# Attention and mixture-of-experts block: scores in tiles of 32 keys, one merging copy for each pair, expert regions in the sorted rows, the first norm on ScalarE, and a new instruction order

## The chip, the cores and the metric

The kernel runs on one core of a Trainium2 chip. The metric is the device time of one launch in microseconds (us), the median of several runs. Engines are called as the profile calls them: PE (TensorE matmul), PEld (its weight loads), DVE (VectorE), ACT (ScalarE), POOL (GpSimd), SP (SyncE, which only issues DMAs here).

## The reference

One transformer block over 4 batches of 1024 tokens, 128 features wide, all in float32:

```python
mod = (silu(c) @ wmod)                      # per batch: sa, ca, ga, sb, cb, gb
h = layernorm(x) * (1 + ca) + sa
# attention: 16 query heads, 4 key/value heads of 64, window of 128 keys, causal
scores = 30 * tanh((q @ k.T) / 8 / 30); mask = (j <= i) & (j > i - 128)
x = x + ga * (softmax(where(mask, scores, -1e30)) @ v) @ Wo.T
h = layernorm(x) * (1 + cb) + sb
# experts: 8, each takes the first C = 512 of the 4096 tokens whose largest gate is its own
gates = softmax(h @ Wg); e = argmax(gates); loc = how many earlier tokens chose e
out_t = gate_t * (relu(h @ W1[e] + b1[e]) @ W2[e] + b2[e]) if loc < 512 else 0
x = x + gb * out
```

## The kernel before

The 4096 tokens are 32 tiles of 128. A tile's queries meet the keys of its own tile and of the tile before it; tiles 0, 8, 16 and 24 (the first of each batch) have no tile before.

**First norm and projections, per pair of tiles.** DVE measures x (`measure1`, `gather1`), POOL makes the reciprocal deviation (`rstd1_of`), DVE writes the normalised tile XN (`normalise1`, L851), PE turns it (`turn_x`), ACT and DVE split it into a high and a low part XH and XL (`high_x`, `full_x`, `low_x`), and PE projects q (four groups), k and v in three float32r passes each (L343 to L345, L373 to L375).

**Scores.** `score(t, h)` makes the scores of one tile for two of its four key/value heads, transposed: keys on partitions, 4 heads by 128 queries in each of two banks. The scores of the own tile go to the two banks `own`, of which there is one pair only; those of the tile before go partly to `own` and partly to two of the six banks `turns` (the use is called "before"), in ten matmuls over 64x64 tiles of the array (L423 to L432). DVE then copies what belongs to the tile before over `own` where a triangular mask says so (`merge`, two predicated copies of 64 partitions, L869). A key of the own tile and one exactly 128 before it share a place, so the probabilities need one set of columns alone. ACT makes tanh (`weigh`, L688) and exp (`expose`, L694); the next `score` waits for that tanh, since it writes the same `own`.

**Weighted values.** `attend(t)` multiplies all probabilities PR by the values of the tile before (V) or by a mix of both tiles (VM, built by two DMAs of SP, `mix_v`), L461, and then adds a correction, the masked probabilities PM (POOL, `mask`, L1224) by the difference VD of the two tiles' values (POOL, `differ`), L468. It does so for the first 32 of each head's 64 value columns and then for the other 32. V matmuls use 128x32 tiles of the array, corrections 64x32 tiles. `sums(t)` (L482) adds up the probabilities, DVE inverts and spreads the sums (`turn_sums`, `invert`, `spread`) and scales (`scale`, L900), ACT and POOL split the result (`high_o` L700, `low_o` L1232), and `out_project` (L495 to L497) works on a pair of tiles.

**Second norm, gates and slots, per tile.** PE turns y back (`turn_y`, L504), DVE adds x (L911), measures, normalises and modulates (L917 to L937), PE turns the result (`turn_h2`, L510) and scores the experts (L516). DVE finds the largest (`top8`, `which`), writes a one-hot row (`mark`, L958), PE counts earlier tokens of the same expert (`count`, L524), DVE reads the count (`locate`, L968), makes slot = expert * 512 + count (`find_slot`, L973), an overflow term that moves a token past the end when its count is 512 or more (`find_over`, L978) and their sum as an integer (`number_slot`, L984). POOL scatters the row to `sorted_rows` by an indirect DMA (`scatter`, L1260); rows past the end are dropped. `sorted_rows` has 4096 rows and is filled with empty rows at the start by one DMA of 6400 KB.

**Experts.** From 433 us on the sorted rows are read back and PE works through the eight experts.

Each engine runs its instructions in the order written. For the first stage that order is written out by hand in one loop an engine, one pass for every two tiles: for instance `for e in range(-4, TILES + 8, 2)` on PE, with calls such as `score(e, 0)` and `attend(e - 2)` in it. Which of the six banks `turns` a use takes stands in the table `HOME`, and PE waits before a use until the bank's former user has read it (`freed`). On SP, `mix_v` waits behind the load of all first expert weights (L274) at the start.

## Time and profile before

| what | us |
|---|---|
| median of 3 runs (508.32 to 510.79) | 510.23 |
| profiled execution, whole | 510.57 |
| its span, first to last instruction | 508.8 |
| PE busy | 434.4 (85%) |
| DVE busy | 367.5 (72%) |
| ACT busy | 286.5 (56%) |
| POOL busy | 287.5 (57%) |

Busy is the time in which at least one instruction of the engine runs. Since one pass of the loops handles two tiles, the first stage repeats itself about every 25 us; a stretch of one such length, looked at instruction by instruction on each engine, says more than the totals. Weight loads overlap the matmuls.

### The profile page before, as it was taken

What the parts mean: (1) busy time and instruction counts of PE and PEld (TensorE: products, weight loads), DVE (VectorE), ACT (ScalarE), POOL (GpSimd) and SP (SyncE); (2) the same over time, 40 slices, a digit from 0 to 9 for tenths busy, and PEclk for the clock granted to TensorE, in tenths of its full rate; (3) what the DMA queues carried; (4) which work ended last, traced back from release to release, by engine and by line L of the source; (5) the groups of instructions that cost most, each with busy time, mean ns of one, the idle gap of its engine ahead of it and who ended that gap; (6) DMA issues with size and microseconds to landing.
All of it is one profiled execution on the core that took longest, in us unless ns stands there. A gap on an engine that the chain in (4) does not pass through costs nothing.

```text
span 508.8 us, 13662 instructions
## 1 busy us (share of the span) xinstructions
PE 434.4 (85%) x4936; PEld 286.6 (56%) x4936; DVE 367.5 (72%) x1061; ACT 286.5 (56%) x505; POOL 287.5 (57%) x398
## 2 busy tenths in 40 slices
PE   2884999899989898999898989989998951699980
PEld 1651666465656565556565655656564541599970
DVE  4272667888998989799989898898778844155541
ACT  3662656576766666665747485747666422455520
POOL 4151547476657575857575757557566853035672
PEclk9997999999999999999999999999999975799995
DMA  9985010101010101001010201020202103991110
GB/s 260 373 277 166 3 27 3 48 6 50 12 55 19 49 19 54 28 23 56 13 59 7 62 11 50 1 65 4 64 11 60 39 26 105 360 329 42 37 42 19
DMA packets 31961, 37.35 MB, mean 73 GB/s; under 512 B 3372, under 2 KB 28267, under 8 KB 31896
## 3 DMA queue, kind: packets, MB, share of 16 engines
q1 hardware_dynamic: 28824, 28.22, 17.9%
q0 software_dynamic: 3072, 8.28, 4.5%
q8 instruction: 40, 0.66, 0.5%
q14 instruction: 25, 0.20, 0.1%
HBM read 15.88 MB, written 17.31 MB: 65 GB/s over the span
## 4 chain that ended last, share of the span: by engine, by line
PE 63%; issue 13%; DVE 13%; DMA 4%; POOL 3%; ACT 2%; another core or an unknown queue 1%; POOLq 0%; SPq 0%; DVEq 0%; ACTq 0%
PE turns L461 7%; PE turns L482 6%; PE own L423 5%; PE turns L343 4%; PE turns L624 4%; PE turns L468 4%; PE turns L345 4%; PE turns L344 4%; PE turns L430 3%; PE turns L495 3%; PE turns L497 2%; PE turns L496 2%; DMA VM<-V 2%; DVE own L869 2%; DVE R L890 2%
## 5 line engine op out<-in xcount | busy, mean ns | idle before, releaser
L1224 POOL TENSOR_SCALAR_AFFINE_SELECT PM<-PR 128x1024 f32<-128x1024 f32 x64 | 70.0, 1094 | 72.3 <-ACT PR L694 72.2
L869 DVE COPY_PREDICATED own<-before,turns 64x512 f32<-64x512 uint32 x112 | 77.9, 695 | 30.7 <-PE own L432 28.6
L1232 POOL TENSOR_TENSOR OL<-O,OH 128x512 fp32r<-128x512 f32 x64 | 80.7, 1284 | 34.1 <-ACT OH L700 33.5
L688 ACT ACTIVATE PR<-own 128x1024 f32<-128x1024 f32 x64 | 65.4, 1021 | 60.4 <-DVE own L869 58.9
L694 ACT ACTIVATE PR<-PR 128x1024 f32<-128x1024 f32 x64 | 67.3, 1054 | 0.5
L423 PE MATMUL own<-Q,K 64*64 64x512 f32 x112 | 59.1, 608 | 8.7 <-DVE PAY L937 4.6
L428 PE MATMUL own<-Q,K 64*64 64x512 f32 x112 | 57.0, 589 | 0.0
L343 PE MATMUL turns<-XH,WqH 128*128 128x256 f32 x128 | 41.7, 325 | 10.7 <-DVE own L869 10.7
L674 ACT ACTIVATE Q<-turns 128x512 f32<-128x512 f32 x64 | 38.4, 603 | 20.8 <-PE turns L345 19.5
L900 DVE TENSOR_TENSOR O<-turns,R 128x512 f32<-128x512 f32 x64 | 41.1, 684 | 12.0 <-PE turns L468 11.4
L1260 POOL DMA_INDIRECT sorted_rows<-PAY,slot_i x32 | 33.7, 1053 | 22.9 <-issue 22.7
L851 DVE TENSOR_SCALAR XN<-x_sb,mv,rstd 128x128 f32<-128x128 f32 x32 | 44.8, 1409 | 0.6 <-POOL rstd L1206 0.6
L461 PE MATMUL turns<-PR,V 128*32 128x256 f32 x448 | 36.6, 399 | 6.4 <-DMA VM<-V 6.4
L700 ACT ACTIVATE OH<-O 128x512 fp32r<-128x512 f32 x64 | 40.8, 640 | 1.2 <-DVE O L900 1.2
L495 PE MATMUL turns<-OH,WoH 128*128 128x256 f32 x128 | 38.5, 300 | 2.4 <-POOL OL L1232 2.4
L468 PE MATMUL turns<-PM,VD 64*32 64x256 f32 x896 | 37.6, 392 | 0.0
L497 PE MATMUL turns<-OH,WoL 128*128 128x256 f32 x128 | 36.7, 287 | 0.0
L496 PE MATMUL turns<-OL,WoH 128*128 128x256 f32 x128 | 36.7, 287 | 0.0
L345 PE MATMUL turns<-XH,WqL 128*128 128x256 f32 x128 | 36.1, 282 | 0.0
L344 PE MATMUL turns<-XL,WqH 128*128 128x256 f32 x128 | 36.1, 282 | 0.0
L424 PE MATMUL own<-Q,K 64*64 64x256 f32 x112 | 36.0, 402 | 0.0
L425 PE MATMUL turns<-Q,K 64*64 64x256 f32 x112 | 36.0, 402 | 0.0
(204 smaller groups left out, 1384.8 us busy)
## 6 DMA issues: line engine op xcount, KB each, us to landing
sorted_rows<-PAY SPq DMA_DIRECT2D x1, 6400.0 KB, 22.9
VM<-V SPq DMA_DIRECT2D x56, 64.0 KB, 2.0
x_sb<-x_dram SPq DMA_DIRECT2D x4, 512.0 KB, 7.7
w_stage<-w_dram SPq DMA_DIRECT2D x1, 2048.0 KB, 11.7
out_dram<-PAY SPq DMA_DIRECT2D x32, 64.0 KB, 2.1
x_sb<-sorted_rows SPq DMA_DIRECT2D x2, 800.0 KB, 9.5
Q<-sorted_rows SPq DMA_DIRECT2D x2, 800.0 KB, 9.9
PR<-sorted_rows SPq DMA_DIRECT2D x2, 800.0 KB
```

Source lines behind the costliest of these rows:

```text
L343: pe.matmul(dst, wh, xh, start=True, stop=False)
L344: pe.matmul(dst, wh, xl, start=False, stop=False)
L345: return pe.matmul(dst, wl, xh, start=False, stop=True)
L423: pe.matmul(scores(0, 0, 0, P), keys(0, t, 0), q(0, 0, P), start=True, stop=True)
L428: pe.matmul(scores(0, 1, 0, P), keys(1, t, 0), q(1, 0, P), start=True, stop=True)
L461: last = pe.matmul(out_of(c, x, g), v[:, d], probabilities(PM if first(t) else PR, slice(0, P), g, c), start=True, stop=first(t), tile_pos ...
L468: last = pe.matmul(out_of(c, x, g), VD[HALVES[c], t % VD_RING, d], probabilities(PM, HALVES[c], g, c), start=False, stop=True, tile_positi ...
L688: act.activation(pr, own[:, :, :].rearrange("p a n -> p (a n)"), ACT.Tanh, scale=SCORE_SCALE).then_inc(tanhed, 1)
L694: act.activation(pr, pr, ACT.Exp, scale=SOFTCAP).then_inc(exped, 1)
L869: dve.copy_predicated(own[mine, :, :].rearrange("p a (r n) -> p (a r) n", n=P)[:, :, mine], before[mine, mine].bitcast(U32).unsqueeze(1).t ...
L1224: pool.affine_select(out=PM[:, u % P_RING, :].rearrange("p (r n) -> p r n", n=P), in_=PR[:, u % P_RING, :].rearrange("p (r n) -> p r n", n ...
L1232: pool.tensor_tensor(OL[:, t % 2, c, :], O[:, t % 2, c, :], OH[:, t % 2, c, :].bitcast(F32), ALU.subtract).then_inc(ol_done, 1)
```

## The change

- Scores: `score` now makes, for the own tile, eight matmuls over 64x32 tiles of the array (32 keys each, only the queries from the first of these keys on), and for the tile before eight more, all into the two banks "before" and in the opposite order of keys. All of it takes place with the array cut the same way.
- `merge` is one predicated copy of 128 partitions by 1024 a call, two calls a tile. For that the banks are cleared once at the start (`banks_cleared`, 128x2048 on DVE).
- `attend` does all V matmuls of a tile first and then all corrections.
- `normalise1` moves from DVE to ACT, as Identity with scale 1/deviation and a bias that POOL makes in two more small instructions for each pair (`minus1`, `shift1`).
- `sorted_rows` has 4096 rows for every expert (32768 in all), of which the first 512 of each are filled with empty rows (eight DMAs of 800 KB in place of one of 6400 KB) and read back. The count starts at expert * 4096, because `seen` starts at 32 * expert in each of 128 partitions; `locate` gives the slot directly, `find_slot` and `find_over` are gone. No row is dropped by the scatter.
- `mark` and `number_slot` move from DVE to POOL.
- The order of all five engines and the table `HOME` are written anew. SP now issues `mix_v(t)` before the stores of older tiles.

```diff
@@ HOME
-    ("before", 0, 0): 2, ("before", 0, 1): 3, ("before", 1, 0): 4, ("before", 1, 1): 1,
-    ("count", 0): 5, ("count", 1): 3,
-    ("h2", 0): 3, ("h2", 1): 0,
-    ("k",): 0,
...
+    ("before", 0, 0): 2, ("before", 0, 1): 2, ("before", 1, 0): 2, ("before", 1, 1): 1,
+    ("count", 0): 2, ("count", 1): 1,
+    ("h2", 0): 4, ("h2", 1): 4,
+    ("k",): 4,
...
@@ score
-                pe.matmul(scores(0, 0, 0, P), keys(0, t, 0), q(0, 0, P), start=True, stop=True)
-                pe.matmul(scores(1, 0, HALF, P), keys(0, t, 1), q(0, HALF, P), start=True, stop=True)
...
+                for lo in range(0, P, B):
+                    for a in range(2):
+                        pe.matmul(own[lo:lo + B, a, :].rearrange("p (r n) -> p r n", n=P)[:, :, lo:P], keys(a, t, lo, lo + B),
+                                  q(a, lo, P), start=True, stop=True, tile_position=(HALF * a, lo))
+                for lo in range(P - B, -1, -B):
+                    for a in range(2):
+                        last = pe.matmul(ps[lo:lo + B, a, :].rearrange("p (r n) -> p r n", n=P)[:, :, 0:lo + B],
+                                         keys(a, t - 1, lo, lo + B), q(a, 0, lo + B), start=True, stop=True,
+                                         tile_position=(HALF * a, lo))
+                last.then_inc(scored, 1)
@@ merge
-                dve.copy_predicated(own[mine, :, :].rearrange("p a (r n) -> p (a r) n", n=P)[:, :, mine],
...
+                dve.copy_predicated(own[:, :, :].rearrange("p a (r n) -> p (a r) n", n=P),
@@ normalise1, now in program_act
+                act.activation(XN[:, j * P:(j + 1) * P], x_sb[:, t, :], ACT.Identity, bias=shift1[:, t:t + 1],
+                               scale=rstd1[:, t:t + 1]).then_inc(normed1, 1)
@@ rstd1_of on POOL
+                pool.tensor_scalar(minus1[:, s], mv1[:, s, 0], -1.0, None, ALU.mult).then_inc(minus1_done, 1)
...
+                pool.tensor_tensor(shift1[:, s], minus1[:, s], rstd1[:, s], ALU.mult).then_inc(shift1_done, 1)
@@ program_pool
+            def mark(t):
+                pool.wait_ge(at_done, t + 1)
+                pool.tensor_scalar(onehot[:, t, :], iota8[:, :], top_at[:, t, 0:1], None, ALU.is_equal).then_inc(one_done, 1)
+
+            def number_slot(t):
+                pool.wait_ge(slot_done, t + 1)
+                pool.tensor_copy(slot_i[:, t:t + 1], slot[:, t:t + 1]).then_inc(slot_i_done, 1)
@@ the loop of PE (its second half)
+                if is_tile(e + 15):
+                    sums(e + 15)
+                if is_tile(e + 18):
+                    project_k(e // 2 + 9)
+                if is_tile(e + 16):
+                    score(e + 16, 1)
+                if is_tile(e + 15):
+                    attend(e + 15)
+                if is_tile(e + 20):
+                    turn_x(e // 2 + 10)
+                if is_tile(e + 17):
+                    score(e + 17, 0)
+                if is_tile(e + 13):
+                    turn_y(e + 13)
```

How the order changes is best seen in three places. The first is PE from the scores of a tile to the weighted values after them, before and then with the change (PR, V, VM, PM and VD are as above):

```order
L423 MATMUL own<-Q,K 64x512 [waits l_kept,xl_done,tanhed]
L424 MATMUL own<-Q,K 64x4x64
L425 MATMUL turns<-Q,K 64x4x64
...
L461 MATMUL turns<-PR,V 32x256 [waits exped,v_kept,vd_done,masked,mixed_in2,sums_turned,q_kept2]
L461 MATMUL turns<-PR,V 32x256 x3
L461 MATMUL turns<-PR,VM 32x256 x4
L468 MATMUL turns<-PM,VD 32x256 x8
L461 MATMUL turns<-PR,V 32x256 x4
L461 MATMUL turns<-PR,VM 32x256 x4
L468 MATMUL turns<-PM,VD 32x256 x8
```

```order
L420 MATMUL own<-Q,K 32x512 [waits merged,slot_done,tanhed]
L420 MATMUL own<-Q,K 32x512
L420 MATMUL own<-Q,K 32x4x96 x2
L420 MATMUL own<-Q,K 32x4x64 x2
L420 MATMUL own<-Q,K 32x4x32 x2
L424 MATMUL turns<-Q,K 32x512 x2
L424 MATMUL turns<-Q,K 32x4x96 x2
L424 MATMUL turns<-Q,K 32x4x64 x2
L424 MATMUL turns<-Q,K 32x4x32 x2
L456 MATMUL turns<-PR,V 32x256 [waits exped,v_kept,vd_done,masked,mixed_in2,sums_turned,l_kept]
...
L456 MATMUL turns<-PR,VM 32x256 x4
L463 MATMUL turns<-PM,VD 32x256 x16
```

There are sixteen score matmuls where there were ten, and the corrections stand in one block of 16 in place of two of 8 with V matmuls between them.

The second is DVE from the transposed sums of an odd tile to the spread of their inverse; `sumsT` and `R` are these, `XN` is the normalised x, `PAY` the row of a token:

```order
L878 STREAM_TRANSPOSE sumsT<-turns 128x512 [waits inverted,summed]
L925 TENSOR_SCALAR turns<-PAY,mv,rstd 128x128 [waits rstd2_done]
L851 TENSOR_SCALAR XN<-x_sb,mv,rstd 128x128 [waits x_turned,rstd1_done]
L884 RECIPROCAL RS<-sumsT 128x16 [waits spread_done,sums_turned]
L933 TENSOR_TENSOR turns<-turns,mod 128x128 [waits n_done]
L869 COPY_PREDICATED own<-before,turns 64x8x64 [waits scored] x2
L890 STREAM_TRANSPOSE R<-RS 128x512 [waits scaled,inverted]
```

```order
L874 STREAM_TRANSPOSE sumsT<-turns 128x512 [waits inverted,summed]
L921 TENSOR_SCALAR turns<-PAY,mv,rstd 128x128 [waits rstd2_done]
L946 MAX_INDEX top_at<-top,logits 128x8 [waits top_done]
L849 BN_AGGR mv<-stats 128x2 [waits stats1_done]
L929 TENSOR_TENSOR turns<-turns,mod 128x128 [waits n_done]
L865 COPY_PREDICATED own<-before,turns 128x1024 [waits scored]
L845 BN_STATS stats<-x_sb 128x6 [waits mv1_done,x_in3]
L880 RECIPROCAL RS<-sumsT 128x16 [waits spread_done,sums_turned]
L886 STREAM_TRANSPOSE R<-RS 128x512 [waits scaled,inverted]
```

The XN instruction ahead of the merge has left DVE, and the reciprocal now stands behind the merge.

The third is POOL, from the slot of a tile to the mask of the next one; with the change the integer slot and the one-hot row are made here:

```order
L1253 COPY PAY<-tok_id 128x1 [waits pay_out2]
L1245 TENSOR_TENSOR seen<-seen,onehot 128x8 [waits seen_done,one_done]
L1253 COPY PAY<-tok_id 128x1 [waits pay_out3]
L1214 TENSOR_TENSOR VD<-V 128x256 [waits pv_done,v_kept]
L1224 AFFINE_SELECT PM<-PR 128x1024 [waits pv_done,exped]
```

```order
L1214 COPY PAY<-tok_id 128x1 [waits pay_out3]
L1196 TENSOR_SCALAR onehot<-iota,top_at 128x8 [waits at_done]
L1221 DMA sorted_rows<-PAY,slot_i 32768x400 [waits g_done,slot_i_done,id_done]
L1177 AFFINE_SELECT PM<-PR 128x1024 [waits pv_done,exped]
L1206 TENSOR_TENSOR seen<-seen,onehot 128x8 [waits seen_done,one_done]
L1200 CAST slot_i<-slot 128x1 [waits slot_done]
L1177 AFFINE_SELECT PM<-PR 128x1024 [waits pv_done,exped]
```

The mask in the last row stands behind an instruction (L1200) that waits for DVE's reading of PE's count.

## Rows read from the trace of the kernel before

**Rows 1.** Span and mean granted clock of the core.
```profile
core 0: 508.8 us, clock 0.956
```

**Rows 2.** Busy time by stretches; length, PE, PEld, DVE, ACT, POOL, clock, DMA.
```profile
249.60:274.70 25.10, 23.45 (x299) 14.70 (x298) 22.48 (x64) 15.64 (x29) 15.91 (x22) 1.00 0.12 34
...
sum 335.00, PE 316.07 PEld 195.78 DVE 287.27 ACT 214.52 POOL 213.35; mean PE 22.58 PEld 13.98 DVE 20.52 ACT 15.32 POOL 15.24
```

**Rows 3.** Waits from 100 to 400 us: who waited for whom, total, times, longest.
```profile
ACT PR L688 <- DVE own L869: 42.7, 18, 4.9
...
PE turns L343 <- DVE own L869: 9.1, 7, 1.3
```

**Rows 4.** Timeline of PE: start, length, line, count, idle time before it.
```profile
261.94 1.07 PE L482 MATMUL turns<-PR,ones 128*32 128x512 f32 x8
263.14 0.61 PE L423 MATMUL own<-Q,K 64*64 64x512 f32 x1
...
263.63 0.38 PE L427 MATMUL own<-Q,K 64*64 64x256 f32 x1
...
263.85 0.38 PE L427 MATMUL own<-Q,K 64*64 64x256 f32 x1
...
264.60 0.64 PE L461 MATMUL turns<-PR,V 128*32 128x256 f32 x8
...
265.60 0.66 PE L468 MATMUL turns<-PM,VD 64*32 64x256 f32 x16
266.19 0.64 PE L461 MATMUL turns<-PR,V 128*32 128x256 f32 x8
...
269.18 0.38 PE L343 MATMUL turns<-XH,WqH 128*128 128x256 f32 x1 [1.32 <-DVE own L869]
```

**Rows 5.** Timeline of DVE over the same stretch.
```profile
264.14 3.30 DVE L851 TENSOR_SCALAR XN<-x_sb,mv,rstd 128x128 f32<-128x128 f32 x1
...
267.71 1.41 DVE L869 COPY_PREDICATED own<-before,turns 64x512 f32<-64x512 uint32 x2
...
270.25 0.33 DVE L851 TENSOR_SCALAR XN<-x_sb,mv,rstd 128x128 f32<-128x128 f32 x1
```

**Rows 6.** Timeline of POOL over the same stretch.
```profile
263.76 1.04 POOL L1260 DMA_INDIRECT sorted_rows<-PAY,slot_i  x1 [0.23 <-issue]
264.83 2.52 POOL L1232 TENSOR_TENSOR OL<-O,OH 128x512 fp32r<-128x512 f32 x2
```

**Rows 7.** Groups by line: shapes, count, busy us, mean ns, idle before and releaser.
```profile
L869 DVE COPY_PREDICATED own<-before,turns 64x512 f32<-64x512 uint32 x112 | 77.9, 695 | 30.7 <-PE own L432 28.6
L688 ACT ACTIVATE PR<-own 128x1024 f32<-128x1024 f32 x64 | 65.4, 1021 | 60.4 <-DVE own L869 58.9 <-PE own L415 1.3
L851 DVE TENSOR_SCALAR XN<-x_sb,mv,rstd 128x128 f32<-128x128 f32 x32 | 44.8, 1409 | 0.6 <-POOL rstd L1206 0.6
L958 DVE TENSOR_SCALAR onehot<-iota,top_at 128x8 bf16<-128x8 f32 x32 | 16.1, 502 | 0.4
L725 ACT ACTIVATE PAY<-mod,gate 128x128 f32<-128x128 f32 x32 | 12.7, 396 | 8.0 <-DVE gate L962 8.0
L1245 POOL TENSOR_TENSOR seen<-seen,onehot 128x8 bf16<-128x8 bf16 x32 | 6.4, 201 | 0.5
```

**Rows 8.** Weight loads of one correction block: min/median/max ns, first and last start.
```profile
L468 PEld LDWEIGHTS turns<-PM,VD x16: 102/104/106, 253.2 to 253.3; 64*32 64x32 f32 x16
```

**Rows 9.** The start: timelines of SP and, last, of PE.
```profile
34.42 0.38 SPq L274 DMA_DIRECT2D w_stage<-w_dram  x1
...
46.69 1.08 PE L461 MATMUL turns<-PR,V 128*32 128x256 f32 x8 [6.41 <-DMA VM<-V]
```

**Rows 10.** The chain that ended last, between the two stages: start, length, what.
```profile
409.86 0.55 PE turns L495
...
419.34 0.46 PE turns L510
...
433.41 1.10 PE turns L603 x4
```

More of the change, by code:

```diff
@@ L151, in build @@
         prod8 = sb("prod8", [P, EXPERTS])
-        loc, slot, over = sb("loc", [P, TILES]), sb("slot", [P, TILES]), sb("over", [P, TILES])
+        slot = sb("slot", [P, TILES])
         slot_i = sb("slot_i", [P, TILES], I32)
@@ L414, in score @@
                         for a in range(2):
-                            last = pe.matmul(scores(half, a, 0, P), keys(a, t, half), q(a, 0, P), start=True, stop=True)
+                            last = pe.matmul(own[HALVES[half], a, :].rearrange("p (r n) -> p r n", n=P),
+                                             keys(a, t, half * HALF, (half + 1) * HALF), q(a, 0, P), start=True, stop=True)
                     last.then_inc(scored, 1)
@@ new lines, in program_pe @@
+            for e in range(-20, TILES - 8, 2):
+                if is_tile(e + 10):
+                    turn_h2(e + 10)
+                if is_tile(e + 16):
+                    project_q(e // 2 + 8, 1)
+                    project_q(e // 2 + 8, 0)
+                    project_q(e // 2 + 8, 3)
+                if is_tile(e + 9):
+                    count(e + 9)
+                if is_tile(e + 14):
+                    sums(e + 14)
+                if is_tile(e + 10):
+                    score_experts(e + 10)
+                if is_tile(e + 15):
+                    score(e + 15, 1)
+                if is_tile(e + 14):
+                    attend(e + 14)
+                if is_tile(e + 16):
+                    project_v(e // 2 + 8)
+                    score(e + 16, 0)
+                if is_tile(e + 12):
+                    out_project(e // 2 + 6)
+                if is_tile(e + 10):
+                    count(e + 10)
+                if is_tile(e + 11):
+                    turn_h2(e + 11)
+                if is_tile(e + 18):
+                    project_q(e // 2 + 9, 2)
+                if is_tile(e + 12):
+                    turn_y(e + 12)
+                if is_tile(e + 11):
+                    score_experts(e + 11)
+                if is_tile(e + 15):
+                    sums(e + 15)
+                if is_tile(e + 18):
+                    project_k(e // 2 + 9)
+                if is_tile(e + 16):
+                    score(e + 16, 1)
+                if is_tile(e + 15):
+                    attend(e + 15)
[5 more added lines that the diff above has]
+                    turn_y(e + 13)
@@ L1130, in program_dve @@
                     full_x(e // 2 + 8)
+                    low_x(e // 2 + 8)
+                if is_tile(e + 9):
+                    add_x(e + 9)
+                if is_tile(e + 7):
+                    invert_gate(e + 7)
+                if is_tile(e + 9):
+                    measure2(e + 9)
+                if is_tile(e + 7):
+                    locate(e + 7)
+                if is_tile(e + 9):
+                    gather2(e + 9)
+                if is_tile(e + 12):
+                    turn_sums(e + 12)
                 if is_tile(e + 8):
                     keep_logits(e + 8)
[L1133 to L1138 removed]
+                if is_tile(e + 22):
+                    gather1(e + 22)
+                if is_tile(e + 12):
+                    invert(e + 12)
                 if is_tile(e + 8):
                     top8(e + 8)
+                    which(e + 8)
+                if is_tile(e + 13):
+                    merge(e + 13, 1)
+                if is_tile(e + 12):
+                    spread(e + 12)
             def low_w1(e):
```

469 lines of the change are left out of this document (176 added, 293 removed).

## Prediction

> **What bounds the kernel now.** First the span and the clock: 508.8 us at a granted clock of 0.956 [rows 1], and the profiled execution took 1.8 us more, 510.6, which is 0.3 above the median of the runs. Then the busy times by stretches: in a pass of the first stage that lasts 25.1 us PE is busy for 23.45 at full clock, DVE for 22.5, ACT and POOL for under 16 each, and over the 14 passes from 56.6 to 391.6 us PE is busy for 316 of 335 [rows 2]. So PE bounds the stage and idles for 18.9 us of it. The waits name the cause: ACT waits 42.7 us for DVE's merge, and PE waits for the same copy in front of L343 [rows 3]. The timelines show why the merge is late. The scores end on PE before 264.60 [rows 4], but DVE has started an XN instruction at 264.14 that takes 3.30 us, where the other of the same form takes 0.33; POOL is meanwhile in a DMA issue and two OL subtractions, 263.76 to 267.35, and DVE goes on 0.1 us after them [rows 5, 6]. The merge starts at 267.71, and PE, which ends the corrections near 267.8, sits until 269.18: 1.3 us, nearly all of what PE loses in the pass. The mean XN takes 1409 ns against 0.33 [rows 5, 7].
>
> The trace shows DVE held by a running POOL instruction. The Trainium skill says so too (SBUF — State Buffer, Who interferes with whom): a tensor_scalar from SBUF to SBUF can take a port pair shared with GpSimd, and the second to issue blocks. By that rule ACT never waits there, so the moved norm would not bring the stall with it.
>
> **The change, part by part.** Names: T is the even tile whose q starts a pass; a pass is two tiles.
>
> *Scores.* A pass of 256 columns holds its part of the array for 0.22 us (L427 at 263.63 and 263.85), and a float32 matmul is two passes [rows 4]. Before, each of the four 64x64 parts gets 512+256 or three times 256 columns, 768, which is 2 x 3 x 0.214 = 1.28; measured, first score to first V matmul, 264.60 - 263.14 = 1.46. So 0.18 goes to draining and refilling. After, each of eight parts gets 512+128 or 384+256 columns, 640: 1.07, with the same 0.17 it is 1.24. That supposes that eight parts run side by side. The corrections, cut the same way, show it: 16 passes on eight parts in 0.59 us [rows 4], their weight loads of 104 ns all started within 0.1 [rows 8]. At that rate per pass, 32 passes take 1.18; at no gain 1.45. I take 1.24, as the column count decides and not the pass count: 56 calls (28 tiles, 2 each) x 0.21 = 11.8 us less.
>
> *Weighted values.* V takes 1.00 (4 passes a part, 0.86, and 0.14), a correction block 0.59 (0.43 and 0.16), twice [rows 4]. With one block of each, two changes of the array's cut are saved, 0.30 a tile, if the 0.15 belongs to the change and not to the passes; if to the passes, nothing. The excess is alike for 8, 16 passes, so it belongs to the change: 28 x 0.30 = 8.4. The new order adds one change of cut a pass (sums, k, scores, where scores followed sums): 15 x 0.15 = 2.3 more.
>
> *XN on ACT.* DVE loses 44.8 us busy [rows 7], most of it being held. ACT gains 32 instructions between 0.28 and 0.40 us (0.396 is L725, the same shape from SBUF with a scale by partition [rows 7]), 0.8 a pass on an engine idle for 9.5. It stands between an exp and a tanh that waits for the merge anyway. POOL gets two more small instructions a pair.
>
> *Merge.* Two copies take 1.41 [rows 5]. One of them, 512 elements a partition, takes 0.70 [rows 7]; one of 1024 lies between that and 1.41, and since the work grows with the elements and one start-up is saved I take 1.2. It shortens the loop scores, merge, tanh, scores by 0.2; it pays only where PE waits.
>
> *Slots.* DVE loses the one-hot (502 ns) and three instructions on one column; POOL gets a one-hot and a cast of about 0.2 each (L1245) [rows 7]: with the norm's two, 1.2 us a pass, which makes 17 of 22 [rows 2]. Queued behind the cast on POOL is a mask, and behind that mask the odd tile's weighted values on PE.
>
> *Laying the new order out by hand* with these durations, PE running without a wait, us from the start of a pass of 22.2: q 0.1, sums 2.45, score(T-1,1) 3.6, values(T-2) 4.85, v 7.75, score(T,0) 8.55, out_project 9.8, count(T-6) 12.75, q2 13.0, turn_y 13.8, sums 14.1, k 15.1, score(T,1) 15.9, values(T-1) 17.15, turn_x 20.05, score(T+1,0) 20.3. The four scores are 4.4 or more apart, and scores, merge and tanh (1.02 [rows 7]) need about 3.7. The narrowest slacks: low_x before count on bank 1, 0.2; the shift of the second norm before turn_x, 0.25; h2T before q0 on bank 4, 0.3; experts 0.3. POOL: DVE reads the count at 13.3, cast, mask(T+1,1) ends at 14.6, wanted at 17.15: 2.5 slack. DVE, without XN, the one-hots and the slots, is busy for about 16 of 22. So nothing but PE is last, and a full pass falls from 25.1 to 25.1 - 1.65 (idle) - 0.84 - 0.60 + 0.15 = 22.2.
>
> *The start.* PE sits 6.4 us before values(1) at 46.69 for VM, whose DMA stands behind the load of L274, issued at 34.42 after the last split [rows 9]. The bytes and the order on SP are the same (eight fills for one), so this barely moves: the load can be issued up to 0.9 us earlier, and one q group (0.7) goes ahead of the wait. The bank clearing on DVE lies under the first loads. 1.2 us less.
>
> *Between the stages.* out_project waits for OL until 409.86, the 31st tile's h2 is queued behind the 30th's at 419.34, and FFN starts at 433.41 [rows 10]. The split chain (scale, OH, OL twice) stays. turn_y(31) now stands ahead of turn_h2(30), which spares about 2 us; the slot chain loses an instruction and gains two hops. 1.5 less. From 433.41 on all is the same.
>
> The sum: idle 18.9, of which I leave 3 for the narrow slacks, 15.9; scores 11.8; values 8.4; added change -2.3; start 1.2; between 1.5; together 36.5. 510.6 - 36.5 = 474.1, on the median 0.3 less: 473.8.
>
> **The rivals.**
>
> *A. The wait only changes its name.* For it: slacks of 0.2 to 0.3 in four places, less than a single small instruction. If three of them are missed by 0.4 us in every pass, 15 x 1.2 = 18 more: 492. Against: DVE now has 6 us a pass to catch up.
>
> *B. Slower: the 64x32 parts don't load side by side.* A score has 32 loads of 0.104 us [rows 8]; one after the other they are 3.3 us against 1.46, 56 x 1.9 = 104 more than now, less the 25 that the rest gives: 590. From 1.9 us a score on (1.24 + 36.5/56) it is slower than before. Against: the correction block takes 0.59, not 16 x 0.104 = 1.7 [rows 4, 8].
>
> The Trainium skill has a rule against small matmuls (TensorE: Matmul & The Clock Gate, Back-to-back issue gap): pairs of load and matmul are sustained at about 81 ns each at 128 columns. It would make 32 passes 2.6 us, 64 more than now on the scores, 550 in all. This trace disagrees for column parts: 37 ns a pass, so I give that rule's result 0.02 of B's chance.
>
> *C. Slower: POOL's chain.* count on PE, locate on DVE, cast and mask on POOL, values on PE. Should POOL, with 17 of 22 us busy and DMA issues among them, run this chain 2.5 us late, PE begins to sit; at 5 us late in every pass 15 x 2.5 = 37 are lost and nothing is won; at 5.5 it is 519. Against: POOL idles for 9 us a pass before [rows 2], and no PE wait on it is among the large ones [rows 3].
>
> *D. It doesn't do what it says*: the scores and values gain nothing (excess belongs to passes), only the wait goes: 510.3 - 15.9 - 2.7 + 2.3 = 494.
>
> **How the numbers follow.** Forecast 0.72; A 0.10, D 0.08 (a mix of both included); B 0.03; C 0.03, and 0.04 for ending within half a per cent of before, which is about what a measurement of this kernel can tell from no change (2.5 us). Predicted 473.8. The central case spans 467 (score 1.18, no idle left, which is 3.4 and 3 less) to 483 (half of the saving on the values, and 5 of idle more). A and D reach 494; with 466 to 489 no more than 2 in 10 is left out. Faster by over 0.5%: 0.90; within: 0.04; slower: 0.06.
>
> **What would show it.** Right: no XN over 0.5 us on any engine; score to V 1.24 us; V block 1.85 and corrections 1.0; passes of 22.2 us, PE busy over 97% of them; DVE under 17 us a pass; values(1) still near 46; the experts' part again 75.4 us from the first L603 on. Wrong: scores over 1.4; a PE wait of over 0.5 us that returns every pass (its releaser names A or C); a first stage shorter by under 25 us.

## The result, and the profile after

| | before | after |
|---|---|---|
| median, us | 509.75 (508.32 to 510.79, 4 runs) | 477.02 (475.98 to 477.41, 4 runs) |
| ratio | | 0.9356, 95% interval 0.9328 to 0.9385 |
| profiled execution, its span | 510.6, 508.8 | 476.8, 475.1 |
| values(1) starts | 46.69 | 45.62 |
| sums(2) starts | 56.58 | 55.09 |
| from sums(2) to sums(31) | 344.99 | 312.77 |
| from sums(31) to the experts' part | 31.84 | 32.27 |
| the experts' part | 75.42 | 74.94 |

sums(t) is the first matmul of the line that adds up the probabilities of tile t (L477 now); the experts' part begins at L596, the turning of the first rows. Of the 33.8 us between the two spans, 32.2 come from the first stage, 1.5 from the start and 0.5 from the experts' part, and 0.4 are given back between the stages.

The busy times of the whole span and, of the view by stretches, one full pass and the first stage's 14 passes (start and end, length, then busy time and instructions of PE, PEld, DVE, ACT and POOL, the granted clock, the DMA share and GB/s), to be read against [rows 2]:

```profile
PE 417.4 (88%) x5608; PEld 294.0 (62%) x5608; DVE 286.9 (60%) x846; ACT 298.0 (63%) x537; POOL 310.8 (65%) x494
...
229.00:250.90 21.90, 21.90 (x350) 14.99 (x348) 16.12 (x50) 16.47 (x31) 16.87 (x29) 1.00 0.13 39
55.10:357.50 302.40, 299.24 (x4566) 201.64 (x4566) 210.11 (x619) 222.53 (x402) 226.21 (x359) 1.00 0.12 36
```

A full pass takes 21.90 us and PE is busy for all of it; over the 14 passes it idles for 3.2 us, where it was 18.9. DVE fell from 22.5 to 16.1 us a pass, and POOL is the busiest of the others. The timeline of PE in one pass, from the sums on (start, duration, line, operation), which answers to [rows 4]:

```profile
229.00 1.07 PE L477 MATMUL turns<-PR,ones 128*32 128x512 f32 x8
230.00 0.39 PE L511 MATMUL turns<-Wg,h2T 128*128 128x8 f32 x2
230.32 0.65 PE L420 MATMUL own<-Q,K 64*32 64x512 f32 x12
...
231.55 0.64 PE L456 MATMUL turns<-PR,V 128*32 128x256 f32 x8
...
233.42 1.09 PE L463 MATMUL turns<-PM,VD 64*32 64x256 f32 x32
234.44 0.39 PE L374 MATMUL turns<-WvH,XH 128*128 128x256 f32 x1
```

From the first score matmul to the first V matmul 1.23 us pass (1.46 before), V takes 1.87 and the corrections 1.02, 2.89 together (3.19 before). The rows of the merge and of the first norm (line, operation, count, busy and mean ns, idle time before and its releaser), against [rows 7]:

```profile
L865 DVE COPY_PREDICATED own<-before,turns 128x1024 f32<-128x1024 uint32 x56 | 68.8, 1229 | 40.3 <-PE turns L424 40.3
...
L642 ACT ACTIVATE XN<-x_sb,shift,rstd 128x128 f32<-128x128 f32 x32 | 13.9, 483 | 0.0
```

The view of the tile XN has the shortest, the median and the longest of the 32, in ns, in the kernel before and in the changed one:

```profile
L851 DVE TENSOR_SCALAR XN<-x_sb,mv,rstd x32: 304/340/3875, 7.8 to 342.8; 128x128 f32<-128x128 f32 x32
```

```profile
L642 ACT ACTIVATE XN<-x_sb,shift,rstd x32: 477/483/489, 9.8 to 301.9; 128x128 f32<-128x128 f32 x32
```

XN takes between 477 and 489 ns in all 32 cases on ACT, where on DVE it took from 0.30 to 3.88 us. Last, the waits from 100 to 370 us (engine, tile and line, what it waited for: us, times, longest), and PE's own over the start and the stage, which answer to [rows 3]:

```profile
ACT PR L689 <- DVE own L865: 34.2, 28, 2.3
DVE own L865 <- PE turns L424: 25.9, 41, 1.7
POOL slot_i L1200 <- DVE slot L961: 24.7, 13, 2.4
...
DVE PAY L907 <- DMA out_dram<-PAY: 5.3, 4, 1.6
```

```profile
PE turns L529 <- DMA w_stage<-wmod_dram: 6.1, 1, 6.1
PE turns L456 <- DMA VM<-V: 6.1, 1, 6.1
PE turns L352 <- ACT XN L642: 1.9, 1, 1.9
...
PE own L420 <- ACT PR L689: 1.7, 3, 0.8
```

ACT still waits 34 us for merges, and DVE now waits for the scores in front of them; none of this reaches PE, whose waits for the merge in the passes are gone. The largest that are left on PE are two waits of 6.1 us at the start, one for the first weights (L529) and one for the first VM.

### The profile page after: what moved, and what is told of

The parts are those of the page before. It is cut to its first block and busy times, and to the rows that moved or that the text cites. A ratio compares the mean times of both kernels' runs of the same rounds, so it can differ in the third digit from the quotient of the medians.

```text
span 475.1 us, 14910 instructions
## 1 busy us (share of the span) xinstructions
PE 417.4 (88%) x5608; PEld 294.0 (62%) x5608; DVE 286.9 (60%) x846; ACT 298.0 (63%) x537; POOL 310.8 (65%) x494
## 5 line engine op out<-in xcount | busy, mean ns | idle before, releaser
L865 DVE COPY_PREDICATED own<-before,turns 128x1024 f32<-128x1024 uint32 x56 | 68.8, 1229 | 40.3 <-PE turns L424 40.3
L689 ACT ACTIVATE PR<-own 128x1024 f32<-128x1024 f32 x64 | 65.5, 1024 | 42.4 <-DVE own L865 42.0
L695 ACT ACTIVATE PR<-PR 128x1024 f32<-128x1024 f32 x64 | 65.8, 1054 | 0.0
L420 PE MATMUL own<-Q,K 64*32 64x256 f32 (+3 forms) x896 | 58.8, 441 | 1.9 <-ACT PR L689 1.7
L424 PE MATMUL turns<-Q,K 64*32 64x128 f32 (+3 forms) x896 | 57.4, 429 | 0.0
L1221 POOL DMA_INDIRECT sorted_rows<-PAY,slot_i x32 | 35.1, 1096 | 14.0 <-issue 10.9
L424 PEld LDWEIGHTS turns<-Q,K 64*32 64x32 f32 x896 | 36.5, 107 | 9.4
L344 PE MATMUL turns<-XH,WqH 128*128 128x256 f32 x128 | 39.2, 307 | 2.0 <-DVE XL L859 1.8
L456 PE MATMUL turns<-PR,VM 128*32 128x256 f32 x448 | 35.8, 388 | 0.0
L463 PE MATMUL turns<-PM,VD 64*32 64x256 f32 x896 | 31.7, 391 | 0.0
L874 DVE STREAM_TRANSPOSE sumsT<-turns 128x512 f32<-128x512 f32 x32 | 22.9, 716 | 13.0 <-PE turns L477 12.2
```

The source lines that it names most:

```text
L344: pe.matmul(dst, wh, xh, start=True, stop=False)
L420: pe.matmul(own[lo:lo + B, a, :].rearrange("p (r n) -> p r n", n=P)[:, :, lo:P], keys(a, t, lo, lo + B), q(a, lo, P), start=True, stop=Tru ...
L424: last = pe.matmul(ps[lo:lo + B, a, :].rearrange("p (r n) -> p r n", n=P)[:, :, 0:lo + B], keys(a, t - 1, lo, lo + B), q(a, 0, lo + B), st ...
L456: last = pe.matmul(out_of(c, x, g), v[:, d], probabilities(PM if first(t) else PR, slice(0, P), g, c), start=(x == 0), stop=(x == 1 and fi ...
L689: act.activation(pr, own[:, :, :].rearrange("p a n -> p (a n)"), ACT.Tanh, scale=SCORE_SCALE).then_inc(tanhed, 1)
L695: act.activation(pr, pr, ACT.Exp, scale=SOFTCAP).then_inc(exped, 1)
```

## The experiments

Each set of runs had the kernel before beside it on the same chip. The sets differ by up to 0.8% (509.93, 505.82 and 508.85 us for the kernel before), so times are compared inside a set, and ratios between sets. The first stage is counted from sums(2) to sums(31), as in the table above. PE's gaps are those of over 80 ns, added up; its idle time is all the time in which no matmul runs.

Each set has one profile of the changed kernel (e8, in the second set, differs from it in the last pass alone). In these three the stage takes 312.8, 309.5 and 311.9 us, with gaps of 4.0, 1.7 and 3.5 us, and sums(2) starts at 55.1, 54.3 and 55.9. So a stage or a start read from two sets can differ by 1 to 3 us with no change in the kernel.

| run | on | median us | ratio to before, interval |
|---|---|---|---|
| e1_interleaved | after | 482.71 | 0.9471 (0.9456 to 0.9487) |
| e2_old_scores | after | 491.88 | 0.9644 (0.9623 to 0.9664) |
| e3_norm_on_dve | after | 523.39 | 1.0277 (1.0254 to 1.0300) |
| e4_before_norm_on_act | before | 492.01 | 0.9646 (0.9623 to 0.9670) |
| e5_before_scores | before | 492.13 | 0.9731 (0.9688 to 0.9775) |
| e6_w1_later | after | 464.41 | 0.9187 (0.9144 to 0.9230) |
| e7_before_all_old_order | before | 471.13 | 0.9308 (0.9268 to 0.9347) |
| e8_tail | after | 471.02 | 0.9321 (0.9279 to 0.9362) |
| g1_after_again | after | 477.40 | 0.9369 (0.9340 to 0.9398) |
| g2_pool_busy | after | 510.65 | 1.0046 (1.0016 to 1.0075) |
| g3_old_order_w1_later | before | 472.55 | 0.9277 (0.9253 to 0.9301) |
| g4_k_before_sums | after | 470.06 | 0.9231 (0.9204 to 0.9258) |

### The first norm: e4 and e3

```diff
@@ e4: the kernel before, XN moved to ACT, nothing else
-                if is_tile(e + 16):
-                    normalise1(e + 16)        # in DVE's loop, and e + 17 likewise
...
+                if is_tile(e - 10):
+                    normalise1(e - 10)        # in ACT's loop, behind expose(e - 15, 1)
+                if is_tile(e - 9):
+                    normalise1(e - 9)
```

> The kernel before with nothing changed but the first norm, which goes to ACT. Theory one (the held XN alone made PE's idle time): the 1.3 us wait in front of L343 goes, most of the 15.9 us is saved, 510 - 13 = 497. Theory two (the order made it, XN was one of several steps between scores and merge): below 5 us saved, 505 to 510. A mean between them says that both have a part.

Measured: 0.9646, 18 us less, 5 more than theory one. The stage is 17.3 us shorter. The view by stretches, from the start of the passes to 370 us:

```profile
56.20:370.00 313.80, 311.45 (x3922) 193.18 (x3921) 248.50 (x768) 223.85 (x398) 216.21 (x312) 1.00 0.12 34
```

PE idles for 2.4 us there; from sums(2) to sums(31) it idles for 3.6, where it was 19.4. With the old order, the old scores and the old slots, this one move takes away nearly all idle time.

e3 is the reverse on the changed kernel: `normalise1` back in DVE's loop, one behind `normalise2(e + 8)`, one behind `shift2(e + 8)` (before, `which(e + 7)` stood between these two).

> The changed kernel with the first norm (XN) as a tensor_scalar on DVE again, between the second norm's steps as before; the two small POOL steps that ACT's form needed stay. XN should again take 0.33 us where POOL pauses and up to 3.3 us where it runs. Theory one (these held instructions were PE's idle time): a merge is late again, about 1 us a pass comes back, 15 x 1.0 = 15 us more, 492, and PE's wait for the merge is again the largest. Theory two (with the new order DVE has 6 us a pass to spare and the scores stand 4.4 us apart, so that it hides a held XN): the XN are as long as before, but the time is within 3 us of 477.

Measured: 523.39, slower than the kernel before. Theory two is out. Theory one is right that the held XN comes back as PE's idle time, but its size is three times too small, and the wait is another one than the merge. The timelines of DVE, of POOL and of PE in e3, around one XN:

```profile
172.73 0.25 DVE L929 TENSOR_TENSOR PAY<-turns,mod 128x128 f32<-128x128 f32 x1
172.91 4.50 DVE L844 TENSOR_SCALAR XN<-x_sb,mv,rstd 128x128 f32<-128x128 f32 x1
177.33 0.28 DVE L833 BATCH_NORM_STATS2 stats<-x_sb 128x6 f32<-128x128 f32 x1
```

```profile
172.42 2.50 POOL L1185 TENSOR_TENSOR OL<-O,OH 128x512 fp32r<-128x512 f32 x2
174.91 0.31 POOL L1196 TENSOR_SCALAR onehot<-iota,top_at 128x8 bf16<-128x8 f32 x1
175.19 2.14 POOL L1177 TENSOR_SCALAR_AFFINE_SELECT PM<-PR 128x1024 f32<-128x1024 f32 x2
```

```profile
177.56 0.66 PE L352 MATMUL turns<-ident,XN 128*128 128x128 f32 x2 [4.33 <-DVE XN L844]
```

And PE's largest wait from 100 to 370 us:

```profile
PE turns L352 <- DVE XN L844: 32.0, 8, 5.2
```

POOL runs two OL, the one-hot and two masks from 172.42 to 177.33, with no gap between them in the rows, and an XN that starts inside that row ends 0.1 us behind it: 4.50 us for 0.33 of work. PE stands 4.33 us in front of `turn_x`. POOL's new order has longer rows without a pause than the old one, so the held instruction became longer (up to 5.1 us, against 3.9), and it is no merge that is late but the turn of x. The Trainium skill's rule on the shared port (SBUF — State Buffer, Who interferes with whom) agrees: the second to issue waits. That it waits for a whole row of instructions, and not for the one that runs, stands in these rows.

The waits are not all of the 46 us. The stage of e3 and that of the changed kernel have the same 4698 matmuls in the trace:

```profile
55.44:413.85 358.41, 321.69 (x4698) 216.51 (x4697) 253.94 (x667) 221.42 (x391) 235.64 (x375) 0.95 0.10 31
177.50:182.00 4.50, 4.44 (x47) 3.18 (x48) 2.62 (x5) 1.65 (x4) 1.79 (x2) 0.66 0.00 0
```

```profile
55.09:367.86 312.77, 308.50 (x4698) 207.84 (x4698) 217.38 (x643) 229.27 (x415) 235.93 (x375) 1.00 0.12 36
```

Of the 45.6 us PE idles for 32.5 and is busy for 13.2 more. Behind the wait of 4.33 us the granted clock is 0.66 on average from 177.5 to 182.0, a mean over its two levels (0.50 is 1.2 GHz, 1.00 is 2.4 GHz), and the score there takes 2.32 us instead of 1.24. So a long wait of PE also slows the matmuls behind it.

### The scores: e5 and e2

```diff
@@ e5: the kernel before with the new score and merge; banks cleared once
...
-                    merge(e + 12, 0, 0)
-                    merge(e + 12, 0, 1)
+                    merge(e + 12, 0)
...
```

> The kernel before with only the sixteen score matmuls of 32 keys and the one merging copy (the banks are cleared once at the start, under the first loads). Theory one (the saving of a score is paid on PE whatever else is late): 56 x 0.23 = 12.9, and the copy that is 0.2 shorter saves 0.2 in each of the 15 passes where PE waits for it, 3 more: 494. Theory two (with XN still on DVE the merge is pinned by the held XN, so that a score that ends 0.23 earlier only makes PE wait longer): under 6 us, 504 to 510, and PE's idle time grows from 17.4 to about 25 of the 315 us from 55 to 370.

Measured: 0.9731, 13.7 us of 505.8 with an interval of 2.2 on either side: theory one. The stage is 14.6 shorter than the one in the table (330.4), but that is read across two sets. XN is still held (mean 1355 ns), but the saving on PE is paid all the same; PE's idle time didn't grow, it is 15.2 of the 315.1 us from 54.9 to 370.

e2 puts the ten matmuls over 64x64 tiles and the two half merges back into the changed kernel.

> The changed kernel with the ten score matmuls of 64 keys and the merge as two half copies. The theory (PE is the bound, every 0.23 us of a score is paid in full) says 56 x (1.46 - 1.23) = 12.9 us more: 489.9, with PE's waits still near 3 us. Rival one, the merge decides: the two copies take 1.41 where one takes 1.23, which makes each of 56 loops from score to tanh 0.2 + 0.2 longer, 22 more, 499, and PE waits in front of the scores. Rival two, other work of the pass was the bound: under 6 us more, below 483.

Measured: 491.88 against 477.0, 14.9 more. A score takes 1.46 us again, so the theory has 12.9 of it. A full pass takes 23.42, 1.5 over the 21.9 of the changed kernel, and four scores give 0.92. Part of the rest is a row that the changed kernel lacks at this place:

```profile
257.39 0.44 PE L352 MATMUL turns<-ident,XN 128*128 128x128 f32 x2 [0.23 <-DVE PAY L940]
```

The half merges end 0.2 later, the second norm's shift stands behind them on DVE, and `turn_x` waits for the bank that it frees. The prediction had a slack of 0.25 at this place. Of the remaining 0.4 a pass, nearly 0.3 lies in the projections of q at the end of the pass, which take 2.50 us to the start of the count behind them instead of 2.22; no gap of over 80 ns stands in them, and the cause is open.

### V and the corrections: e1

```diff
@@ e1: the changed kernel, in attend
...
-                if not first(t):
-                    for x in range(2):
-                        for g in range(KV):
+                    if first(t):
+                        continue
+                    for g in range(KV):
...
```

The V matmuls of the second half of the columns start their own accumulation again, as before.

> The changed kernel with the V matmuls and the corrections in turn again (V, corrections, V, corrections in each tile that has them). The theory says that about 0.15 us is lost at each change between the array cut by column quarters and cut in eight, so the two changes that come back cost 28 tiles x 0.30 = 8.4 us: 477.0 + 8.4 = 485.4, and the values of a tile take 3.19 us again where they take 2.89 now. The rival (the excess over 0.214 us a pass belongs to the matmuls themselves) says 477.0, values at 2.89.

Measured: 482.71, 5.7 more. On PE the values take 3.19 us again (233.52 to 236.71) and the stretches are 1.00, 0.59, 1.00, 0.60, so the 0.15 of a change of cut is real, and two of them cost 0.30 a tile. A full pass takes 22.48 us in place of 21.88. The stage is 5.8 us longer: PE is busy for 7.1 us more (26 of the 28 tiles fall into it, which is 7.8 at 0.30) and idles for 1.3 less. Three profiles of the changed kernel differ by more than that in their gaps (4.0, 3.5 and 1.7 us, against 2.7 in e1), so it isn't shown that the faster order has waits which the slower one hid. What is missing between 8.4 and 5.7 stays open.

### Order, banks and slots: e7, with e8 beside it

e7 is the kernel before with the three parts above (XN on ACT, scores and merge, V before corrections) and none of the rest: the old order on all engines, the old banks, slots and one-hots on DVE, one empty region. e8 is the changed kernel but for one instruction of the last pass, and serves as its measure on the same chip.

> The kernel before with three parts of the change, the first norm on ACT, the scores of 32 keys with one merging copy, and V with the corrections last, but with the order on all engines, the six banks, the one-hot and the slots as before. Theory one (the parts add, and the new order and the slots are worth nothing by themselves): 492.0 - 12.9 - 8.4 = 470.7, up to 473 with waits of 2 us. Theory two (a pass of 22 us needs the new order, the old one leaves merges and banks late): 477 or more; 482 if each pass waits 0.7 us.

Measured: 471.13 beside 471.02. The number of theory one assumed 510 us for the kernel before; on this chip, in ratio, 0.9308 is 474.6 of 509.9, between the 473 of theory one and the 477 of theory two. So the parts add up to nearly what they should, and a pass of 22 us doesn't need the new order: the new order, the table of banks, the regions of all tokens and the one-hots on POOL, taken together, are worth nothing that can be measured in the total. A full pass of e7 takes 21.74 us, one of the changed kernel 21.88; that is the change of cut which the new order adds (sums, k, scores). The first stage is 308.6 against 309.5, and sums(2) starts at 58.09 against 54.30: the new order is better at the start by what it loses later (in the medians; the two profiled spans, 470.9 and 468.8, differ by 2.1). Which of its four parts gives and which takes was not separated. So what the prediction laid out by hand for the new order would have held with the old.

### The narrow slacks: g2

```diff
@@ g2: the changed kernel, ahead of mask(e + 9, 1) on POOL
+                    for n in range(3):
+                        pool.affine_select(out=spare[...], in_=zeros[...], ...)
```

> The changed kernel with three more POOL instructions of about 1.07 us each a pass (a mask of constants written to a tensor that nobody reads), behind the cast of the even tile's slot and ahead of the mask of the odd tile. The trace of the changed kernel has that mask done at 241.15 us and wanted at 243.84, so 2.7 us of slack, and POOL idle for 4.7 of 21.9 us. Theory (the chain of count, locate, cast and mask is what POOL's work can make late): 3.2 - 2.7 = 0.5 us a pass, 14 passes, 7 more: 1.5% over the changed kernel. Rival one (something else queued on POOL, the second norm's steps or an OL, has less slack): 15 us more or over. Rival two (slack is larger than it looks, since PE's order lets everything shift): within 2 us.

Measured: 510.65 against 477.40 on the same chip, 33 us more: rival one. The waits of g2 from 100 to 370 us, of all engines and of PE:

```profile
DVE turns L922 <- POOL rstd L1193: 30.1, 11, 2.9
```

```profile
PE turns L457 <- issue: 8.3, 11, 1.0
PE turns L353 <- DVE PAY L934: 7.0, 7, 1.1
PE turns L478 <- POOL PM L1178: 5.6, 3, 1.9
```

Two things are late. The odd tile's mask is, as computed: PE stands 0.8 us ahead of the values (L457; 0.5 was expected), and the row names no releaser, but a mask ends 0.2 us ahead of each. Then the second norm: DVE waits up to 2.9 us for the reciprocal deviation, queued on POOL behind the same mask, and `turn_x` waits 1.07 for the shift. A full pass takes 23.9 us, and 4.6 us more are lost between the stages (36.85). So 2.7 us is the slack of one chain; the smallest slack behind POOL is that of the second norm.

### The start: e6, g4 and g3

```diff
@@ e6: program_sp of the changed kernel; w1_in is awaited at 16 * EXPERTS
-            sp.dma_start(w1_sb, w1.rearrange("e h f -> h e f")).then_inc(w1_in, 16)
...
+                if 0 <= e + 16 < 2 * EXPERTS:
+                    n = e // 2 + 8
...
+                    sp.dma_start(w1_sb[:, n, :], w1[n]).then_inc(w1_in, 16)
```

> The changed kernel with the 2048 KB load of the experts' first weights, which stands on SP ahead of the first copies for VM and was issued at 34.20 us, cut into eight loads of 256 KB, each behind the copies of a later pair of tiles. PE idles 6.10 us at 39.5 to 45.6 us for VM. Theory one (VM waits behind that load in the DMA queues): the idle time goes, and so does a spell at the slow clock behind it, 477.0 - 6.1 - 1 = 470. Theory two (VM waits for other things, the eight fills or the second norm's rows, or the next wait is right behind): below 2 us saved, 475 to 477. Loads that fall beside VM copies later could cost 0.2 us in each of eight passes: 1.6 more.

Measured: 464.41 beside 471.02 (e8), 6.6 less. values(1) starts at 40.19 in place of 45.72, and sums(2) at 47.08 in place of 54.30. In the view of PE's waits from 20 to 60 us the VM row is gone:

```profile
PE own L423 <- ACT PR L692: 0.8, 1, 0.8
PE own L416 <- ACT PR L692: 0.7, 1, 0.7
PE turns L347 <- DVE O L899: 0.2, 1, 0.2
```

Theory one: VM waited behind that load. The stage is 0.7 longer (310.3 against 309.5).

The start gains more than the wait, which is 5.4 us in e8: sums(2) is 7.2 earlier, and from values(1) to sums(2) it takes 6.89 us instead of 8.58. In e8 PE runs at the lower level of its clock behind the wait, in e6 at the upper one (the views of e8 and e6 from 46 to 49 us):

```profile
46.00:49.00 3.00, 3.00 (x32) 1.35 (x24) 0.00 (x0) 0.00 (x0) 0.61 (x1) 0.50 0.03 5
```

```profile
46.00:49.00 3.00, 3.00 (x47) 1.81 (x48) 1.80 (x6) 3.00 (x6) 1.82 (x2) 1.00 0.00 0
```

g4 adds to this a changed place of one call, `project_k` ahead of the odd tile's `sums`, so that sums and scores stand together.

> The changed kernel with the experts' first weights in eight later parts and with the projection of k put ahead of the odd tile's sums, so that sums and scores stand side by side again and one change of the array's cut is spared in each pass. Theory (a change of cut costs about 0.15): 15 x 0.15 = 2.2 us less than with the weights alone, a full pass at 21.73 where it is 21.88, ratio 0.9187 - 0.0044 = 0.914. Rival (DVE's turn of the sums comes 0.9 us later and something behind it is late): a wait of PE appears and the ratio is 0.919 or more.

Measured: 470.06 beside 477.40 (g1), 7.3 less; its ratio, 0.9231, is not below the 0.9187 of e6. The expectation's rival holds. A full pass without gaps takes 21.79 (133.40 to 155.19), 0.09 less than the changed kernel, so there is a gain a pass, but smaller than 0.15, and the gaps grew. Among its waits is one that g1 has with 3.0 us in two times:

```profile
DVE PAY L910 <- DMA out_dram<-PAY: 14.0, 8, 2.7
```

DVE waits there for the stores of x. That the later loads lengthen these waits is shown by e6 and e8, which differ in the loads (and in one instruction of the last pass): 9.9 us in six times against 2.8 in two, from 50 to 370 us. Every run in the old order has none. What the loads do to the stores was not followed.

> The kernel before with the three parts (first norm on ACT, scores of 32 keys with one merging copy, V and the corrections apart) in the old order, and the experts' first weights loaded in eight parts behind later VM copies. The parts should add: ratio 0.9308 to the kernel before, less 8.7 of 510, is 0.914. If the old order was one that waited for VM for some other reason, 0.925 or more.

Measured: 0.9277, 4.9 us less than g1. The parts didn't add: the first VM came early (values(1) at 40.84), but the stage took 315.9 us, 4.0 more than g1's 311.9, with PE gaps of 0.7 us in front of L514, the experts' scores, in four passes. The expectation (0.914) missed. The later loads disturb the old order more than the new: 1.6 us are gained on e7 by the ratios, where the new order gains 6.8 (e6 beside e8). g4 and g3 were on one chip, and their executions don't overlap (468.9 to 471.1 and 471.7 to 473.6): 2.5 us for the new order, with k moved. So the new order, worth nothing in the comparison with e7, is worth something once the start is mended.

> The changed kernel again, unedited, so that the three beside it can be compared with it on one chip: 0.9356 of the kernel before, as in the first measurement.

Measured: 0.9369, within the first interval.

### Between the stages: e8

```diff
@@ e8: POOL, last pass only
-                if is_tile(e + 4):
+                if is_tile(e + 4) and e + 5 != LAST:
                     scatter(e + 4)
...
+                if e + 5 == LAST:
+                    scatter(e + 4)            # behind mark(31), no longer ahead of it
```

> The changed kernel with the last one-hot on POOL (tile 31) ahead of the scatter of tile 30, in the last pass only. Theory (the one-hot waits 1 us behind that scatter's issue, and the chain of the last slot starts from it): from the last which to the first row load 1 us less, 476.0. Rival (the scatter of tile 30 then goes out later and the rows wait for it): no change, 477.0. The rest of the run is the same, so the stretch between the stages in the trace tells it and not the total.

POOL's timeline in the changed kernel, from the scatter of tile 30 to that of tile 31, and in e8:

```profile
391.08 1.00 POOL L1221 DMA_INDIRECT sorted_rows<-PAY,slot_i  x1 [0.83 <-POOL slot_i L1200]
392.14 0.31 POOL L1196 TENSOR_SCALAR onehot<-iota,top_at 128x8 bf16<-128x8 f32 x1
392.53 0.20 POOL L1206 TENSOR_TENSOR seen<-seen,onehot 128x8 bf16<-128x8 bf16 x1
393.02 0.58 POOL L1200 CAST slot_i<-slot 128x1 int32<-128x1 f32 x1 [0.29 <-DVE slot L961]
394.44 1.07 POOL L1221 DMA_INDIRECT sorted_rows<-PAY,slot_i  x1 [0.84 <-issue]
```

```profile
387.09 0.32 POOL L1196 TENSOR_SCALAR onehot<-iota,top_at 128x8 bf16<-128x8 f32 x1 [1.16 <-DVE top_at L946]
387.87 1.06 POOL L1221 DMA_INDIRECT sorted_rows<-PAY,slot_i  x1 [0.46 <-issue]
388.96 0.23 POOL L1206 TENSOR_TENSOR seen<-seen,onehot 128x8 bf16<-128x8 bf16 x1
389.15 0.64 POOL L1200 CAST slot_i<-slot 128x1 int32<-128x1 f32 x1
390.62 1.00 POOL L1221 DMA_INDIRECT sorted_rows<-PAY,slot_i  x1 [0.83 <-issue]
```

The one-hot starts earlier, but now the scatter of tile 30 stands between it and the cast. From the last `which` to the last scatter it was 3.32 us (391.12 to 394.44) and is 3.80: no gain, as the rival had it, and half a microsecond lost. The scatter's issue and the steps of the last slot are on one engine, and both orders pay for it.

The cast in this chain is long, 0.58 and 0.64 us where it takes 0.18 in the passes, and DVE's timeline in the changed kernel shows what runs beside it:

```profile
392.87 1.29 DVE L1093 TENSOR_TENSOR WqL<-w_stage,WqH 128x512 fp32r<-128x512 f32 x2
```

The first of these two ends at 393.56 and the cast, started at 393.02, at 393.61; in e8 the second ends at 389.75 and the cast at 389.79; g1 repeats the changed kernel's. That looks like the hold of XN the other way round: a POOL instruction ends 0.04 us behind the DVE instruction beside which it started. It is argued from these rows alone; no run moved L1093 away.

## Why the prediction was right, point by point

The forecast of 473.8 us stands beside 477.0, 3.2 less than measured and inside 466 to 489. In spans 36.5 us were forecast and 33.8 came: 1.6 less from the stage and 1.9 less between the stages, 0.3 more at the start and 0.5 from the experts' part, for which nothing was forecast.

**What bounds the kernel.** That PE bounds the stage, and that its idle time came from an XN held by POOL, is shown by e4, which moves XN alone: 17.3 us of stage, for which the prediction had 15.9.

**Scores.** 1.24 us was predicted and 1.23 measured. The cost by columns, on eight parts side by side, holds. At 11.8 us the term was small: 56 x 0.23 is 12.9, and alone it was worth 13.7 (e5), taken back 14.9 (e2). In e2 the half merges, which the prediction took for hidden, are late for `turn_x`; in e5 the difference from 12.9 is inside the interval. Rival B (590 us) and the rule of the Trainium skill beside it (TensorE: Matmul & The Clock Gate, Back-to-back issue gap) are out for these parts of the array: 32 passes in 1.23 us are 38 ns each, not 81.

**Weighted values.** 1.85 and 1.0 were predicted, 1.87 and 1.02 measured, and e1 brings back 3.19. The term of 8.4 us is right by the tile and worth 5.7 in time when taken back; the difference was not explained.

**XN on ACT.** 0.28 to 0.40 us was predicted, 0.48 measured; ACT has the room, and nobody waits for it in the passes. This move was not only useful but needed: under the new order on POOL, XN on DVE costs 46 us (e3), 13 of them by a lower clock behind the waits.

**The new order.** The hand-made layout gave passes of 22.2 us; they take 21.9. The added change of cut is there (21.88 against 21.74 in e7). The prediction leaned on the layout to show that no other wait comes up, and that was right; but e7 shows that the old order would have had none either. The narrow slacks named there are real: the second norm's shift in front of `turn_x` is the place where both e2 and g2 begin to wait.

**Rivals A and D.** No wait of PE comes back in every pass: the gaps of the stage add up to 4.0 us, for which 3 were left, and none is over 0.8. Both the scores and the values gained (e5, e1), so D is out as well.

**Rival C.** The chain of count, locate, cast and mask ran as laid out: 13.4 us from the start of the pass for the cast, 14.6 for the end of the mask (239.92 and 241.15; the pass begins 2.45 ahead of the sums at 229.00). The rival's point from which it decides, 2.5 us, was that chain's alone. g2 shows that 3.2 us more on POOL at that place cost 33 us, nearly five times the 7 us that this chain was to give, because the second norm is queued on POOL behind the same mask.

**The start.** 1.2 less was predicted and 1.5 measured, but the changed kernel's sums(2) starts anywhere from 54.3 to 55.9 in its three profiles, so that the size agrees is partly luck. The wait for VM stayed at 6.1 us, as said.

**Between the stages: the step that failed.** The prediction said 1.5 us less; it was 0.4 more. Two terms were mis-sized. `turn_y(31)` ahead of `turn_h2(30)` "spares about 2 us": from h2(30) to h2(31) it was 4.29 us and is 3.35, so 0.9. And the slot chain, which "loses an instruction and gains two hops", took 2.32 us from the last `which` to the last scatter and takes 3.32. The hops were priced as hops, and two things on POOL were left out: the one-hot starts 0.8 us later, behind the issue of tile 30's scatter (1.0 us), and the cast takes 0.4 longer beside L1093 of DVE. Against them, the step from one-hot to cast is 0.25 shorter. In the passes this is hidden, in the last one nothing hides it. The one other order tried (e8) is no better. These two terms cancel; of the 0.4 us that the whole lost, 0.2 lies in the DMAs from the last scatter to the first rows (5.69 us for 5.47).

**The sum.** The stage was to become 33.8 us shorter (15.9 + 11.8 + 8.4 - 2.3) and became 32.2. The parts alone give more (17.3, 14.6 in the stage, 5.8), 37.7, less 2.1 for the change of cut: 35.6. Why 3.4 us are missing isn't settled. The parts may share idle time that each takes away; but the 14.6 was measured in the second set, in which the changed kernel's stage is itself 3.2 us shorter (309.5), and this alone would explain it.

## What to carry to other kernels

- An instruction that another engine holds back costs by the longest row of work without a pause on that engine, not by its mean. Look for one form of instruction with very different durations (0.33 and 3.30 us in one pass here) and move it to an engine that isn't held. That was worth 18 of the 33 us of a change of which the diff shows mostly other things.
- When a step moves to another engine, price what is queued in front of it there, and price it once more for the last pass, where nothing hides it. Of several chains through that engine the one with the smallest slack decides, not the one that was moved.
- A load that isn't needed for long, issued ahead of a small one that is, can cost more than a clever reordering: the eight smaller loads gave 6.6 us, the new order nothing that shows in the total by itself and 2.5 us, with k moved, beside these loads. That wait of 5.4 us cost more than itself, since the matmuls behind it ran at the lower clock.

## What the runs showed of the hardware that was not expected

- A DVE tensor_scalar of 0.33 us lasted 4.50 us and up to 5.1 while POOL went from instruction to instruction without a pause; 0.1 us behind the end of POOL's row it was done, in all nine cases of over 0.5 us in e3 and all twelve in the kernel before.
- A change of how the array is cut between 128x32 and 64x32 tiles costs 0.15 us (e1, two changes, 0.30). The change spared by g4, between sums and the whole array, gave 0.09.
- The hold seems to go the other way too: the cast of one column, 0.18 us on POOL in the passes, took 0.58 and 0.64 as the last one before the last scatter, and in three traces ended 0.04 us behind the end of a DVE tensor_tensor (L1093).
- Behind a wait of PE for VM of 5.4 us the granted clock was 0.50 from 46 to 49 us (e8), and 1.00 in e6, which has no such wait. Behind the seven waits of 4.3 to 5.2 us in e3 it fell too, and the same 4698 matmuls took 13.2 us more. In g2, whose waits of PE are at most 1.9 us, it stayed at 1.00 over the stage.
